# A shifted-window attention and convolution block on one core: maximum of the scores issued ahead of the normalization steps on DVE, probability copy issued ahead of exp on ACT

## The chip, the core and the metric

One core of a Trainium2 chip runs the whole program in one launch. The time is the device time in microseconds. The kernel before took 3653.8 us as the median of three runs (3641.2 to 3657.81). The engines are PE (matrix products, with PEld as its weight loads), DVE (vector), ACT (scalar functions and copies), POOL (a second elementwise engine) and SP, which only issues DMA transfers. Each works through its own list of instructions in the order written, and semaphores hold an instruction until another engine's work is done.

## The reference

For each of 32 images of 56 x 56 x 128 values:

```python
x = x + swin_attention(group_norm(x))   # 7x7 windows shifted by 3, 8 heads of 16 channels
x = x + conv3x3(group_norm(x))          # weights: scaled signs times a pruning mask

# inside the attention, for each of the 64 windows of 49 tokens
q, k, v = split(tokens @ qkv_weight.T + qkv_bias)
attn = softmax(q @ k.T / 4 + relative_position_bias + shift_mask)
out  = (attn @ v) @ proj_weight.T + proj_bias
```

## The kernel before

An image has 8 rows of 8 windows. A row is cut into 4 units, one for each pair of heads, so that an image has 32 units and the program runs 32 x 32 = 1024 of them. Every engine's list is written as a loop over images and, in it, over the unit number `u` from 0 to 31. What an engine does in a step of that loop is fixed by `u`; several images are in work at once: the attention of one, the convolution and the second normalization of the one before, and the loads and the first normalization of the next.

One unit `g` goes through these stations. PE forms the scores of two units together (`scores`, L908). DVE adds the bias into `s_sb` (L766, waits for `scores_ready`) and takes the row maximum `s_max` (L771). POOL subtracts it (L443). ACT takes exp into `probs` (L498, in the step after), PE turns it (`probsT_ps`, L919, two steps after), ACT copies the turned probabilities out of PSUM (`probsT`, L505, the same step as the turn). `probs` has two buffers, so exp of a unit also waits until the unit two before it has been turned.

One row of windows then closes a loop over engines. Let s0, s1, s2, s3 be the steps with `u % 4` equal to 0, 1, 2, 3.
- In s1, at its end, PE does the projection of a row (`misc_ps`, L895, needs `oT_lo`) and then `values` of the next row: 64 products with `v` (L932) and 32 sums of probabilities (L936), both into `attn_ps`. `values` needs the last `probsT` copy of its row (L505), which ACT makes in the same s1.
- In s2 PE goes on with `scores` of two units, and DVE takes the reciprocal of the sums (`recip`, L746, needs `attn_ps`). SP writes `recip` to DRAM (L366) and reads it back spread over partitions into `recip_wide` (L371).
- In s0, DVE multiplies into `o_sb` (L751, needs `recip_wide`), ACT forms the high half `oT_hi` (L548), and in s1 DVE forms the low half `oT_lo` (L759). That lets the projection go.

Around these stand, in fixed steps, DVE's low halves for the convolution and for the tokens (`plane_lo`, L778; `tok_lo`, L856), the sums of the convolution (L787 to L848), statistics, and the addition of the projection to `x` (L809), which waits for PE. ACT's list in a step is exp, then in s2 `m_1` of the convolution (L539), then the `probsT` copy, then the rest (`oT_hi`, copies of q, k, v, of loads and stores). No scheduler is at work: an engine does the next thing of its list or waits.

## Time and profile before

| | before |
|---|---|
| median of three runs | 3653.8 us (3641.2 to 3657.81) |
| the profiled execution | 3636.98 us |
| its span | 3635.2 us |
| PE busy | 3190.5 us (88%) |
| DVE busy | 3073.1 us (85%) |
| ACT busy | 2555.1 us (70%) |
| POOL busy | 2365.1 us (65%) |
| granted TensorE clock | 0.983 |

The span is what lies between the first and the last recorded instruction; the profiled execution's own time is 1.8 us longer. A busy share is a mean over all stages and over all of the span. Idle time in front of an instruction is put down to what released it. In the middle of the span the work repeats from image to image: the products of L932 for the same row of windows start at 1854.34 us and again at 1961.12 us, which is 106.78 us for an image.

### The profile page before, as it was taken

The numbers are of one execution on the slowest core, as the hardware profiler recorded it, in microseconds if no ns is written. First come the engines' busy times: TensorE is split into PE (matmuls) and PEld (weight loads), VectorE is DVE, ScalarE is ACT, GpSimd is POOL, SyncE is SP. The second block draws the span as 40 slices with busy tenths as digits, with TensorE's granted clock in tenths as the row PEclk, the third lists the DMA queues.
The fourth block names the chain that finished last, engine by engine and source line by source line (L and its number), as shares of the span: only waits on it lengthen the run. The fifth ranks groups of instructions, "written<-read, shape, count | busy, mean of one in ns | idle before, by whom it ended". The sixth has DMA issues, their size and how long they took to land.

```text
span 3635.2 us, 155064 instructions
## 1 busy us (share of the span) xinstructions
PE 3190.5 (88%) x64395; PEld 2684.8 (74%) x64395; DVE 3073.1 (85%) x6399; ACT 2555.1 (70%) x5729; POOL 2365.1 (65%) x3683
## 2 busy tenths in 40 slices
PE   2889989889899899898899999889898899898896
PEld 1667777777777777777777777777777777787775
DVE  5689888888888888888888888888888898888895
ACT  1667777767677777777777777777677777777772
POOL 4466666766667666667766667766667666667763
PEclk9999999999999999999999999999999999999998
DMA  2111111111111111111111111111111111111111
GB/s 57 37 42 52 47 42 47 49 50 49 37 47 50 49 52 47 42 47 50 52 52 50 42 45 49 50 52 50 37 47 50 50 52 47 42 47 50 34 35 36
DMA packets 260489, 169.26 MB, mean 47 GB/s; under 512 B 23120, under 2 KB 259792, under 8 KB 259792
## 3 DMA queue, kind: packets, MB, share of 16 engines
q1 hardware_dynamic: 259792, 159.34, 15.9%
q8 instruction: 514, 8.42, 1.0%
q14 instruction: 183, 1.50, 0.1%
HBM read 104.69 MB, written 54.59 MB: 44 GB/s over the span
## 4 chain that ended last, share of the span: by engine, by line
PE 33%; DVE 32%; issue 13%; POOL 9%; DMA 8%; ACT 4%; SPq 0%; DVEq 0%; ACTq 0%; POOLq 0%
PE conv_ps L1014 8%; DVE s_sb L766 6%; PE qkv_ps L895 6%; DMA recip_wide<-recip_dram 5%; PE attn_ps L932 4%; PE scores_ps L908 4%; PE attn_ps L936 4%; DVE plane_lo L778 3%; POOL s_sb L443 3%; DVE s_max L771 3%; DMA recip_dram<-recip 3%; DVE oT_lo L759 3%; PE probsT_ps L919 3%; DVE tok_lo L856 3%; DVE recip L746 2%
## 5 line engine op out<-in xcount | busy, mean ns | idle before, releaser
L443 POOL TENSOR_TENSOR s_sb<-s_sb,s_max 113x392 f32<-113x392 f32 x1024 | 998.9, 975 | 1092.7 <-DVE s_max L771 1091.4
L505 ACT COPY probsT<-probsT_ps 128x392 f32<-128x392 f32 x1024 | 490.8, 479 | 376.6 <-PE probsT_ps L919 366.4
L498 ACT ACTIVATE probs<-s_sb 113x392 f32<-113x392 f32 x1024 | 552.4, 539 | 221.1 <-POOL s_sb L443 218.6
L470 POOL TENSOR_TENSOR plane<-x_n 128x224 f32<-128x224 f32 x896 | 656.4, 753 | 18.7
L919 PE MATMUL probsT_ps<-ident,probs 113*128 113x113 f32 x4096 | 585.0, 265 | 38.7 <-ACT probsT L505 35.3
L771 DVE TENSOR_REDUCE s_max<-s_sb 113x8 f32<-113x392 f32 x1024 | 574.9, 561 | 35.3
L766 DVE TENSOR_TENSOR s_sb<-scores_ps,bias 113x392 f32<-113x392 f32 x1024 | 565.8, 552 | 41.0 <-PE scores_ps L908 37.1
L569 ACT COPY v<-qkv_ps 64x256 f32<-64x256 f32 (+2 forms) x1280 | 391.0, 325 | 211.6 <-PE qkv_ps L895 205.5
L1014 PE MATMUL conv_ps<-plane_hi,wc_hi 128*128 128x224 f16 x2688 | 484.4, 263 | 23.1 <-DVE conv_y L840 19.0
L919 PEld LDWEIGHTS probsT_ps<-ident,probs 113*128 113x128 f32 x4096 | 433.5, 141 | 90.7 <-ACT probs L498 47.9
L908 PE MATMUL scores_ps<-k,q 32*49 32x98 f32 x16384 | 477.4, 252 | 19.7 <-issue 19.4
L1014 PE MATMUL conv_ps<-plane_hi,wc_lo 128*128 128x224 f16 x2688 | 479.4, 261 | 0.0
L1014 PE MATMUL conv_ps<-plane_lo,wc_hi 128*128 128x224 f16 x2688 | 410.1, 262 | 34.9 <-DVE plane_lo L778 34.9
L908 PEld LDWEIGHTS scores_ps<-k,q 32*49 32x49 f32 x16384 | 365.6, 121 | 90.4 <-issue 32.6
L895 PE MATMUL qkv_ps<-wT_hi,tok_hi 128*128 128x128 f16 (+1 forms) x2304 | 395.6, 226 | 3.7 <-ACT v L569 1.9
L895 PE MATMUL qkv_ps<-wT_hi,tok_lo 128*128 128x128 f16 (+1 forms) x2304 | 389.1, 220 | 1.7 <-issue 1.7
L895 PE MATMUL qkv_ps<-wT_lo,tok_hi 128*128 128x128 f16 (+1 forms) x2304 | 389.1, 220 | 0.4 <-issue 0.3
L932 PEld LDWEIGHTS attn_ps<-probsT,v 128*32 128x32 f32 x16384 | 208.5, 113 | 218.5 <-ACT probsT L505 190.6
L932 PE MATMUL attn_ps<-probsT,v 128*32 128x49 f32 x16384 | 244.8, 213 | 129.7 <-ACT probsT L505 128.8
L482 POOL TENSOR_SCALAR x_n<-x,gn_y,gn_shift 128x371 f32<-128x371 f32 (+2 forms) x576 | 347.4, 613 | 7.6 <-POOL gn_shift L432 7.6
L746 DVE RECIPROCAL recip<-attn_ps 128x98 f32<-128x98 f32 x256 | 195.7, 765 | 162.9 <-PE attn_ps L936 162.6
L560 ACT ACTIVATE k<-qkv_ps,k_bias,k_scale 128x392 f32<-128x392 f32 x512 | 322.9, 687 | 4.5 <-PE qkv_ps L895 4.4
(144 smaller groups left out, 6799.1 us busy)
## 6 DMA issues: line engine op xcount, KB each, us to landing
x_in<-in_x_dram SPq DMA_DIRECT2D x224, 224.0 KB, 3.9
recip_wide<-recip_dram SPq DMA_DIRECT2D x256, 196.0 KB
out_dram<-x_out SPq DMA_DIRECT2D x224, 224.0 KB, 2.3
recip_dram<-recip SPq DMA_DIRECT2D x256, 12.2 KB, 1.7
x<-in_L_conv_w_dram SPq DMA_DIRECT2D x1, 576.0 KB
x<-L_conv_pruning_mask_dram SPq DMA_DIRECT2D x1, 576.0 KB
x_n<-_conv_rel_pos_table_dram SPq DMA_DIRECT2D x14, 10.7 KB
x_n<-in_mask_dram SPq DMA_DIRECT2D x1, 196.0 KB
```

Of the source, the lines that this page charges most:

```text
L443: nc.gpsimd.tensor_tensor(s, s, top, ALU.subtract).then_inc(sub_ready, 1)
L470: last = nc.gpsimd.tensor_tensor(plane[:, t % 2, j], *sums[j])
L498: nc.scalar.activation(probs[0:QP, slot % 2, :, :, 0:N], s_sb[0:QP, slot % 4], ACT.Exp)\
L505: nc.scalar.copy(probsT[:, g % PT_SLOTS], probsT_ps[:].rearrange("p (w n) -> p w n", n=ODD)[:, :, 0:N])\
L569: last = nc.scalar.copy(v[half, slot, w0:w0 + n, :, e * HD:(e + 1) * HD], vals[half, b:b + n, :, e, :])
L766: vec.tensor_tensor(s_sb[0:QP, u % 4].rearrange("p w h m -> p (w h m)"), scores_ps[0:QP, u % 2, 0:WP * 2 * N], bias[0:QP, edge, u % PAIRS] ...
L771: vec.tensor_reduce(s_max[0:QP, u % 4], s_sb[0:QP, u % 4].rearrange("p w h m -> p (w h) m"), AX.X, ALU.max).then_inc(max_ready, 1)
L895: last = mm(out_ps, w, t, start=(n == 0), stop=(n == 2))
L908: last = mm(scores_ps[p0:p0 + N, (u + n) % 2, (w // 2) * 2 * N:(w // 2 + 1) * 2 * N], q[at, r % 2, w, :], k[at, r % 2, w].rearrange("p e m ...
L919: last = nc.tensor.transpose(probsT_ps[:, w * 128:w * 128 + QP], probs[0:QP, u % 2, w].rearrange("p e m -> p (e m)"), ident[0:QP, 0:QP])
L932: mm(attn_ps[parts, w * N:(w + 1) * N], v[:, row % 2, w, pair, :], probsT[:, (row * PAIRS + pair) % PT_SLOTS, w, :], start=True, stop=True)
L1014: last = mm(conv_ps[:, j, 0:PP].rearrange("p (r w) -> p r w", w=W), w[:, j * KW + dx, :], p[:, j, k * TPAIRS:(k + 1) * TPAIRS, dx:dx + W], ...
```

## The change

On DVE, the two instructions of a unit's scores (bias and maximum) now stand at the head of each step, and the reciprocal (in s2), the product (in s0) and the low half (in s1) behind them. On ACT, the copy of the turned probabilities stands at the head of each step, ahead of exp and of `m_1`. No instruction is added or removed, and PE's, POOL's and SP's lists are the same.

```diff
--- before.py
+++ after.py
@@ -525,6 +525,8 @@
 
             def body(i):
                 for u in range(UNITS):
+                    if live(i, 0 if u >= LAG_T else -1):
+                        evacuate_probsT(i, i * UNITS + (u - LAG_T), u - LAG_T)
                     if live(i, 0 if u >= 1 else -1):
                         exp_unit(i, i * UNITS + (u - 1), u - 1)
                     for t in range(TILES):
@@ -538,8 +540,6 @@
                                 act.wait_ge(scaled_bias_ready, 1)
                             nc.scalar.activation(m_1[:], conv_ps[:, 1, 0:PP], ACT.Identity, bias=scaled_bias[:])\
                                 .then_inc(m1_ready, 1)
-                    if live(i, 0 if u >= LAG_T else -1):
-                        evacuate_probsT(i, i * UNITS + (u - LAG_T), u - LAG_T)
                     row = row_of(i, u, NORMED_AT)
                     if row is not None:
 
@@ -738,25 +738,6 @@
             def body(i):
                 for u in range(UNITS):
 
-                    row = row_of(i, u, VALUES_AT + 1)
-                    if row is not None:
-
-                        dve.wait_ge(attn_ready, row + 1)
-                        need(dve, recip_out, 16 * row)
-                        vec.reciprocal(recip[:], attn_ps[:, RT:RT + SUM_COLS]).then_inc(recip_ready, 1)
-                    row = row_of(i, u, NORMED_AT)
-                    if row is not None:
-
-                        dve.wait_ge(recip_wide_in, 16 * (row + 1))
-                        vec.tensor_tensor(o_sb[:].rearrange("p r (w c) -> p w r c", c=WIN),
-                                          attn_ps[:, 0:RT].rearrange("p (w r c) -> p w r c", r=WIN, c=WIN),
-                                          recip_wide[:].rearrange("p (w r c) -> p w r c", r=WIN, c=WIN), ALU.mult)\
-                            .then_inc(o_ready, 1)
-                    row = row_of(i, u, SPLIT_AT)
-                    if row is not None:
-
-                        dve.wait_ge(oT_hi_ready, row + 1)
-                        vec.tensor_tensor(flat(oT_lo), flat(o_sb), flat(oT_hi), ALU.subtract).then_inc(oT_lo_ready, 1)
                     if live(i):
 
                         g = i * UNITS + u
@@ -770,6 +751,25 @@
                         dve.wait_ge(biased, g + 1)
                         vec.tensor_reduce(s_max[0:QP, u % 4], s_sb[0:QP, u % 4].rearrange("p w h m -> p (w h) m"),
                                           AX.X, ALU.max).then_inc(max_ready, 1)
+                    row = row_of(i, u, VALUES_AT + 1)
+                    if row is not None:
+
+                        dve.wait_ge(attn_ready, row + 1)
+                        need(dve, recip_out, 16 * row)
+                        vec.reciprocal(recip[:], attn_ps[:, RT:RT + SUM_COLS]).then_inc(recip_ready, 1)
+                    row = row_of(i, u, NORMED_AT)
+                    if row is not None:
+
+                        dve.wait_ge(recip_wide_in, 16 * (row + 1))
+                        vec.tensor_tensor(o_sb[:].rearrange("p r (w c) -> p w r c", c=WIN),
+                                          attn_ps[:, 0:RT].rearrange("p (w r c) -> p w r c", r=WIN, c=WIN),
+                                          recip_wide[:].rearrange("p (w r c) -> p w r c", r=WIN, c=WIN), ALU.mult)\
+                            .then_inc(o_ready, 1)
+                    row = row_of(i, u, SPLIT_AT)
+                    if row is not None:
+
+                        dve.wait_ge(oT_hi_ready, row + 1)
+                        vec.tensor_tensor(flat(oT_lo), flat(o_sb), flat(oT_hi), ALU.subtract).then_inc(oT_lo_ready, 1)
                     t, half = divmod(u - VLO_AT, 2)
                     if 0 <= t < TILES and live(i, -1):
 
```

The first place is DVE, in a stretch of s0, s1 and s2 of one row: from the step that makes the product `o_sb` to the step that takes the reciprocal of the next row. Before:

```order
L751 TENSOR_TENSOR o_sb<-attn_ps,recip_wide 128x8x7x7 [waits recip_wide_in]
L766 TENSOR_TENSOR s_sb<-scores_ps,bias 113x392 [waits probs_ready,scores_ready]
L771 TENSOR_REDUCE s_max<-s_sb 113x8 [waits biased]
L778 TENSOR_TENSOR plane_lo<-plane,plane_hi 128x2x4x56 [waits plane_hi_ready]
L759 TENSOR_TENSOR oT_lo<-o_sb,oT_hi 128x392 [waits oT_hi_ready]
L766 TENSOR_TENSOR s_sb<-scores_ps,bias 113x392 [waits probs_ready,scores_ready]
L771 TENSOR_REDUCE s_max<-s_sb 113x8 [waits biased]
L778 TENSOR_TENSOR plane_lo<-plane,plane_hi 128x2x4x56 [waits plane_hi_ready]
L809 SCALAR_TENSOR_TENSOR x<-misc_ps,w_max,x 128x7x53 [waits misc_ready]
L809 SCALAR_TENSOR_TENSOR x<-misc_ps,w_max,x 128x7x3
L815 BN_STATS gn_stats<-x 128x6 [waits misc_free]
L746 RECIPROCAL recip<-attn_ps 128x98 [waits recip_out,attn_ready]
```

And the same stretch of the changed kernel, with the two instructions of s2 that now stand ahead of the reciprocal left to the second place:

```order
L747 TENSOR_TENSOR s_sb<-scores_ps,bias 113x392 [waits probs_ready,scores_ready]
L752 TENSOR_REDUCE s_max<-s_sb 113x8 [waits biased]
L764 TENSOR_TENSOR o_sb<-attn_ps,recip_wide 128x8x7x7 [waits recip_wide_in]
L778 TENSOR_TENSOR plane_lo<-plane,plane_hi 128x2x4x56 [waits plane_hi_ready]
L747 TENSOR_TENSOR s_sb<-scores_ps,bias 113x392 [waits probs_ready,scores_ready]
L752 TENSOR_REDUCE s_max<-s_sb 113x8 [waits biased]
L772 TENSOR_TENSOR oT_lo<-o_sb,oT_hi 128x392 [waits oT_hi_ready]
L778 TENSOR_TENSOR plane_lo<-plane,plane_hi 128x2x4x56 [waits plane_hi_ready]
L809 SCALAR_TENSOR_TENSOR x<-misc_ps,w_max,x 128x7x53 [waits misc_ready]
```

The product and the low half each moved behind the bias and maximum of their step; between the low half and the addition to `x`, which waits for the projection, the two score instructions are gone.

The second place is DVE at the reciprocal, in s2 of the row that follows. Before:

```order
L815 BN_STATS gn_stats<-x 128x6 [waits misc_free]
L746 RECIPROCAL recip<-attn_ps 128x98 [waits recip_out,attn_ready]
L766 TENSOR_TENSOR s_sb<-scores_ps,bias 113x392 [waits probs_ready,scores_ready]
L771 TENSOR_REDUCE s_max<-s_sb 113x8 [waits biased]
L787 TENSOR_TENSOR m_sum<-m,conv_ps 128x224 [waits conv_sums,m1_ready]
```

Now:

```order
L815 BN_STATS gn_stats<-x 128x6 [waits misc_free]
L747 TENSOR_TENSOR s_sb<-scores_ps,bias 113x392 [waits probs_ready,scores_ready]
L752 TENSOR_REDUCE s_max<-s_sb 113x8 [waits biased]
L759 RECIPROCAL recip<-attn_ps 128x98 [waits recip_out,attn_ready]
L787 TENSOR_TENSOR m_sum<-m,conv_ps 128x224 [waits conv_sums,m1_ready]
```

The reciprocal waits for the sums, which PE finishes ahead of the scores; it now stands behind the instruction that waits for the scores.

The third place is ACT in s1 and s2 of the same image. Before:

```order
L498 ACTIVATE probs<-s_sb 113x8x49 [waits probsT_ready,sub_ready]
L505 COPY probsT<-probsT_ps 128x392 [waits attn_ready,probsT_ready]
L560 ACTIVATE k<-qkv_ps,k_bias,k_scale 128x8x49 [waits qkv_ready]
L560 ACTIVATE k<-qkv_ps,k_bias,k_scale 128x8x49
L498 ACTIVATE probs<-s_sb 113x8x49 [waits probsT_ready,sub_ready]
L539 ACTIVATE m<-conv_ps,scaled_bias 128x224 [waits conv_sums,conv_half]
L505 COPY probsT<-probsT_ps 128x392 [waits attn_ready,probsT_ready]
```

Now:

```order
L505 COPY probsT<-probsT_ps 128x392 [waits attn_ready,probsT_ready]
L498 ACTIVATE probs<-s_sb 113x8x49 [waits probsT_ready,sub_ready]
L560 ACTIVATE k<-qkv_ps,k_bias,k_scale 128x8x49 [waits qkv_ready]
L560 ACTIVATE k<-qkv_ps,k_bias,k_scale 128x8x49
L505 COPY probsT<-probsT_ps 128x392 [waits attn_ready,probsT_ready]
L498 ACTIVATE probs<-s_sb 113x8x49 [waits probsT_ready,sub_ready]
L541 ACTIVATE m<-conv_ps,scaled_bias 128x224 [waits conv_sums,conv_half]
```

The copy no longer stands behind exp and `m_1`, and these two stand behind the copy's wait for the turn on PE.

## Rows read from the trace of the kernel before

**Rows 1.** The page's busy times: engine, us (share of the span), instructions.

```profile
PE 3190.5 (88%) x64395; PEld 2684.8 (74%) x64395; DVE 3073.1 (85%) x6399; ACT 2555.1 (70%) x5729; POOL 2365.1 (65%) x3683
```

**Rows 2.** The page's chain that ended last, shares of the span by engine.

```profile
PE 33%; DVE 32%; issue 13%; POOL 9%; DMA 8%; ACT 4%; SPq 0%; DVEq 0%; ACTq 0%; POOLq 0%
```

**Rows 3.** The waits: who <- whom: us in total, times, longest.

```profile
ACT probsT L505 <- PE probsT_ps L919: 366.4, 227, 3.4
...
DVE recip L746 <- PE attn_ps L936: 162.6, 105, 4.3
PE attn_ps L932 <- ACT probsT L505: 128.8, 69, 3.4
...
DVE o_sb L751 <- DMA recip_wide<-recip_dram: 103.0, 78, 3.5
...
PE misc_ps L895 <- DVE oT_lo L759: 23.5, 56, 2.6
```

**Rows 4.** Stretches between starts of L932: length, busy us (instructions), clock, DMA.

```profile
1854.34:1867.43 13.09, 11.09 (x239) 8.92 (x239) 9.07 (x17) 9.80 (x23) 12.17 (x24) 1.00 0.21 56
1867.43:1881.50 14.07, 13.71 (x269) 11.96 (x269) 13.35 (x28) 12.39 (x29) 13.14 (x16) 1.00 0.37 91
1881.50:1896.28 14.78, 13.04 (x259) 10.88 (x258) 14.00 (x28) 11.47 (x26) 12.02 (x16) 1.00 0.20 56
1896.28:1911.58 15.30, 12.12 (x255) 10.56 (x255) 13.46 (x32) 8.86 (x21) 12.00 (x27) 1.00 0.11 32
1911.58:1923.94 12.36, 12.05 (x252) 10.35 (x252) 10.49 (x19) 10.45 (x24) 8.84 (x13) 1.00 0.13 38
1923.94:1936.51 12.57, 12.12 (x253) 10.27 (x252) 12.36 (x24) 9.84 (x23) 7.04 (x11) 1.00 0.13 38
1936.51:1948.41 11.90, 11.90 (x253) 10.41 (x253) 9.80 (x21) 8.42 (x20) 4.18 (x5) 1.00 0.13 39
1948.41:1961.12 12.71, 10.92 (x239) 8.91 (x238) 11.98 (x34) 8.44 (x20) 3.80 (x8) 1.00 0.13 38
```

**Rows 5.** Timeline of DVE, fifth stretch: start, us, instruction, idle before.

```profile
1913.24 0.77 DVE L746 RECIPROCAL recip<-attn_ps 128x98 f32<-128x98 f32 x1 [3.09 <-PE attn_ps L936]
1914.05 0.57 DVE L766 TENSOR_TENSOR s_sb<-scores_ps,bias 113x392 f32<-113x392 f32 x1
...
1915.42 1.14 DVE L856 TENSOR_TENSOR tok_lo<-x_n,tok_hi 128x392 f16<-128x392 f32 x1
...
1922.00 1.21 DVE L759 TENSOR_TENSOR oT_lo<-o_sb,oT_hi 128x392 f16<-128x392 f32 x1
```

**Rows 6.** Timeline of PE: the projection of the fifth stretch; `values` after the eighth.

```profile
1923.35 0.33 PE L895 MATMUL misc_ps<-oT_hi,wT_hi 128*128 128x392 f16 x1 [0.31 <-DVE oT_lo L759]
...
1961.12 0.92 PE L932 MATMUL attn_ps<-probsT,v 128*32 128x49 f32 x64 [0.86 <-ACT probsT L505]
```

**Rows 7.** Timeline of DVE, first stretch.

```profile
1856.01 0.77 DVE L746 RECIPROCAL recip<-attn_ps 128x98 f32<-128x98 f32 x1 [1.02 <-PE attn_ps L936]
...
1862.46 0.57 DVE L751 TENSOR_TENSOR o_sb<-attn_ps,recip_wide 128x392 f32<-128x392 f32 x1 [1.85 <-DMA recip_wide<-recip_dram]
...
1864.01 0.69 DVE L778 TENSOR_TENSOR plane_lo<-plane,plane_hi 128x448 f16<-128x448 f32 x1
```

**Rows 8.** Timeline of DVE, seventh stretch.

```profile
1938.50 0.76 DVE L746 RECIPROCAL recip<-attn_ps 128x98 f32<-128x98 f32 x1
...
1944.60 0.57 DVE L751 TENSOR_TENSOR o_sb<-attn_ps,recip_wide 128x392 f32<-128x392 f32 x1 [0.62 <-DMA recip_wide<-recip_dram]
...
1946.15 0.56 DVE L759 TENSOR_TENSOR oT_lo<-o_sb,oT_hi 128x392 f16<-128x392 f32 x1
```

**Rows 9.** Timeline of POOL and of ACT, end of the fourth stretch.

```profile
1902.66 1.15 POOL L443 TENSOR_TENSOR s_sb<-s_sb,s_max 113x392 f32<-113x392 f32 x1 [0.26 <-DVE s_max L771]
...
1910.62 0.54 ACT L498 ACTIVATE probs<-s_sb 113x392 f32<-113x392 f32 x1 [0.26 <-POOL s_sb L443]
1911.06 0.46 ACT L505 COPY probsT<-probsT_ps 128x392 f32<-128x392 f32 x1
```

More of the change, by code:

```diff
@@ L739, in body @@
                 for u in range(UNITS):
+                    if live(i):
+                        g = i * UNITS + u
+                        dve.wait_ge(scores_ready, g + 1)
+                        need(dve, probs_ready, g - 3)
+                        edge = int(u // PAIRS == ROWS - 1)
+                        vec.tensor_tensor(s_sb[0:QP, u % 4].rearrange("p w h m -> p (w h m)"),
+                                          scores_ps[0:QP, u % 2, 0:WP * 2 * N],
+                                          bias[0:QP, edge, u % PAIRS].rearrange("p w h m -> p (w h m)"), ALU.add)\
+                            .then_inc(biased, 1)
+                        dve.wait_ge(biased, g + 1)
+                        vec.tensor_reduce(s_max[0:QP, u % 4], s_sb[0:QP, u % 4].rearrange("p w h m -> p (w h) m"),
+                                          AX.X, ALU.max).then_inc(max_ready, 1)
                     row = row_of(i, u, VALUES_AT + 1)
@@ L759, in body @@
                         vec.tensor_tensor(flat(oT_lo), flat(o_sb), flat(oT_hi), ALU.subtract).then_inc(oT_lo_ready, 1)
-                    if live(i):
-                        g = i * UNITS + u
-                        dve.wait_ge(scores_ready, g + 1)
-                        need(dve, probs_ready, g - 3)
-                        edge = int(u // PAIRS == ROWS - 1)
-                        vec.tensor_tensor(s_sb[0:QP, u % 4].rearrange("p w h m -> p (w h m)"),
-                                          scores_ps[0:QP, u % 2, 0:WP * 2 * N],
-                                          bias[0:QP, edge, u % PAIRS].rearrange("p w h m -> p (w h m)"), ALU.add)\
-                            .then_inc(biased, 1)
-                        dve.wait_ge(biased, g + 1)
-                        vec.tensor_reduce(s_max[0:QP, u % 4], s_sb[0:QP, u % 4].rearrange("p w h m -> p (w h) m"),
-                                          AX.X, ALU.max).then_inc(max_ready, 1)
                     t, half = divmod(u - VLO_AT, 2)
```

## The prediction, made before the changed kernel was run

> **What bounds the kernel now.** I read the busy shares first: PE 88%, DVE 85% [rows 1]. Neither is full, so something passes between them. The chain of waits says the same: 33% PE, 32% DVE, 8% DMA [rows 2]. Then the list of waits, for the places at which the change touches two engines. DVE waits at the reciprocal for the sums 105 times of 256 (162.6 us); PE waits at `values` for the probability copy (128.8 us); DVE waits at the product for the transfer of the reciprocals (103.0 us, 78 times); PE waits at the projection for the low half 56 times, though only for 23.5 us [rows 3]. Last the stretches of one image, cut at the starts of `values` [rows 4]; I call them A to H. They add to 106.78 us. The reader is to see that no one engine bounds them all: PE is busy for the whole of G (11.90 of 11.90), DVE for nearly all of F (12.36 of 12.57), and D, the longest, has neither full.
>
> All of them share one loop: sums on PE, reciprocal on DVE, DRAM and back, product, low half, projection, and `values` again. The change moves three links of that loop behind two instructions each, so I price the loop first and go through the stretches after it.
>
> **The durations.** With t the start of `values`:
> - t to the start of bias in s2 is 2.47 (1911.58 to 1914.05) when DVE isn't late; the reciprocal of 0.77 stands inside that gap, at t + 1.66, while PE is still at the scores [rows 4, 5]. In A it is 1856.01, t + 1.67 [rows 7].
> - o_sb, bias and maximum take 1.55 from start to start, in A (1862.46 to 1864.01) and in G (1944.60 to 1946.15). A product takes about 0.48 of it before the next starts, an estimate from its 0.57, so bias and maximum take 1.07 [rows 7, 8].
> - From the end of the reciprocal to the product, where the product really waited, 5.68 in A (1856.78 to 1862.46) and 5.34 in G (1939.26 to 1944.60) [rows 7, 8].
> - From the end of the low half to the next `values`, where PE waited for it, 0.73 (1923.21 to 1923.94) [rows 4 to 6].
> - The low half takes 0.56 in G and 1.21 in E [rows 5, 8].
>
> **The change, part by part.**
>
> 1. Reciprocal behind bias and maximum (s2). Where DVE came early, the reciprocal used PE's 0.8 us at the scores. Now DVE idles through that gap, and the reciprocal ends at t + 2.47 + 1.07 + 0.77 = t + 4.31 instead of t + 2.43: 1.88 later. Nothing hides this for the transfer.
>
> 2. Product behind bias and maximum (s0). Where the product waits for the transfer, the two now run inside that wait: -1.07 for what follows them, nothing for the product.
>
> 3. Low half behind bias and maximum (s1). The projection comes 1.07 later where PE waits for it. Bias and maximum used to cover DVE's wait for the projection; now DVE has nothing (or one `plane_lo`) there.
>
> So the loop through the transfer is at least 2.47 + 1.07 + 0.77 + 5.34 + 1.55 + 0.56 + 0.73 = 12.49, and 12.8 to 13.4 with 5.68 or with a `plane_lo` or `tok_lo` in s0. The loop through DVE's work is what DVE does from bias of s2 to the end of the low half, plus 0.73 + 2.47 = 3.20 for projection, `values` and scores, under which only the 1.3 to 1.9 us of additions and statistics fit. Before, all of DVE's work fitted.
>
> 4. Whether DVE and POOL hold each other up. `oT_lo` takes 1.21 just after POOL has begun a subtraction and 0.56 otherwise, and `tok_lo` 1.14 [rows 5, 8]. Behind its own unit's maximum, `oT_lo` starts before POOL does, as it does in G; so I take 0.65 off in C and E and 0.58 off E's `tok_lo` in s2, which the reciprocal now parts from the maximum. E's `tok_lo` in s0 moves behind the product, while POOL subtracts: +0.35, an estimate (0.84 of subtraction less 0.48). The Trainium skill has this as a rule (page "SBUF — State Buffer", section "Who interferes with whom"): a DVE instruction with two SBUF inputs and a reading GpSimd instruction exclude each other, and the first to issue decides who waits. By that rule these savings are sure; without it E and C would be 0.9 and 0.6 slower still. The trace agrees, with 0.56 against 1.21.
>
> 5. The copy ahead of exp. At the end of D the copy stood behind exp, which waited 0.26 for POOL and held it 0.44 more (1910.62 to 1911.06) [rows 9]: -0.70. At the end of H `values` waited 0.86 for the copy [rows 6]: -0.86. Of PE's 128.8 us at this wait [rows 3] the rest, up to 3.2 us an image, is the wait for POOL's normalization in D, and stays. The price: in s2 exp and `m_1` now stand behind ACT's wait for the turn (366.4 us in all [rows 3]). That puts them about 0.8 to 2 us later. Exp of that unit is needed a whole step later, and `m_1` only by a DVE that is itself later, so I cost it at nothing but in B, where ACT also serves PE's input tiles through one buffer. If that cover is gone, each row pays up to 0.4.
>
> **The sum, stretch by stretch.**
> - A (13.09): the product starts at t + 4.31 + 5.68 = t + 9.99, before it was t + 8.12. Bias and maximum are then done, so `plane_lo`, for which PE's convolution waits, starts at t + 10.47 instead of t + 9.67. +0.8.
> - B (14.07): DVE busy 13.35, of it 1.9 behind the low half: 13.2 to 13.35 - 1.9 + 3.2 = 14.5 to 14.65. +0.5.
> - C (14.78): DVE busy 14.00; the gap of 0.8 is added, 0.65 comes off the low half. +0.2.
> - D (15.30): bounded by POOL, whose last subtraction before the normalization waits for a DVE maximum [rows 9]; this comes 0.7 later, and the copy gives 0.70 back. 0.
> - E (12.36): bias to end of the low half was 9.16; with reciprocal 0.77, bias and maximum 1.07, less 0.65 and 0.58, plus 0.35, 10.1. 2.47 + 10.1 + 0.73 = 13.3. +0.95.
> - F (12.57): the same work, but here DVE came late to the reciprocal, so part of the gap was idle for it already; both loops give about 13.1. +0.5.
> - G (11.90): the transfer loop, 12.49. +0.6.
> - H (12.71): the loop through DVE gives 12.9 (busy 11.98 less about 2.3 of additions and statistics, plus 3.2), after the 0.86 is used up. +0.2.
>
> Together +3.75 us an image, 32 images: +120 us. The profiled execution took 3636.98, so the changed one should take 3757. The median of the runs is 3653.8, 17 above that execution, which gives 3774. I say 3768.
>
> **The rivals.**
> - ACT's order costs too: exp and `m_1` late in s2 hold up PE's next turn or the input tiles' buffer in most rows, 0.4 us x 256 = 100 more: 3870. For it: 366.4 us of waiting in front of the copy. Against it: the need of those results is a step away. 0.13.
> - Faster. The low half and the product have slack on PE (only 23.5 us of waiting in 56 of 256 rows), the scores get to POOL, ACT and `values` sooner, and what is left is part 5 (1.56 x 32 = 50) and some of part 4: 3595. It would need the 1.07 at the low half to be covered by PE's other work in nearly all rows, and it decides the sign from the point where the projection would have waited anyway. Against it: PE already waits there in E, and G's PE has no gap to give. 0.07.
> - The rows take up most of the delays. DVE comes late to the reciprocal in 151 of 256 rows, so it loses no gap there, and part 5 balances the rest: 3650 to 3690, centre 3665. 0.15, of which half is within 0.5%.
> - That the lists don't move as said can't be: the order shows it.
>
> **How the numbers follow.** The forecast (3700 to 3820) has 0.65, the larger loss 0.13, the absorbed one 0.15, the faster one 0.07. The range leaves out the faster case and the far part of the larger loss: 3665 to 3840. A difference below 0.5% (18 us) can't be told from none here. Slower: 0.65 + 0.13 + half of 0.15, about 0.86; within 0.5% 0.07; faster 0.07.
>
> **What would show it.** Right: DVE's bias instruction now waits for the scores in over 100 rows, with some 0.6 to 0.8 us each; the wait of the projection for the low half grows from 23.5 us to over 100; DVE's wait for the projection grows; the reciprocal waits for nothing; the product waits for the transfer in more rows, A and G among them; PE's wait at `values` falls by 30 to 50 us; `oT_lo` takes near 0.6 on average. E and G are longer by 0.6 to 1. Wrong: if the projection hardly waits for the low half, part 3 is wrong and the time is near that of before; if PE's wait at the turns grows, part 5 was priced too low.

## The result, and the profile after

The changed kernel takes 3911.95 us (median of four runs, 3899.91 to 3914.53) against 3650.52 of before: 1.071 times as long, 95% interval 1.068 to 1.075. The forecast was slower, with 3768 us in a range of 3665 to 3840; the loss is 261 us where about 120 were forecast. The profiled execution's span is 3898.1 us.

The page's busy times and chain by engine, after [rows 1, 2]:

```profile
PE 3250.1 (83%) x64395; PEld 2674.6 (69%) x64395; DVE 3105.9 (80%) x6399; ACT 2494.3 (64%) x5729; POOL 2352.6 (60%) x3683
...
PE 31%; DVE 30%; DMA 16%; issue 13%; POOL 6%; ACT 5%; SPq 0%; ACTq 0%; DVEq 0%; POOLq 0%
```

No instruction was added, and what every engine is busy with changed by 2.4% or less; the engines wait more, and DMA's share of the chain doubled from 8% to 16%. The waits after (who <- whom: us in total, times, longest) [rows 3]:

```profile
ACT probsT L505 <- PE probsT_ps L919: 659.9, 391, 4.0
ACT oT_hi L548 <- DVE o_sb L764: 443.1, 256, 8.6
DVE s_sb L747 <- PE scores_ps L908: 278.7, 246, 4.5
...
PE qkv_ps L895 <- ACT q L557: 217.1, 164, 4.5
DVE x L809 <- PE misc_ps L895: 175.8, 185, 2.2
DVE o_sb L764 <- DMA recip_wide<-recip_dram: 167.9, 113, 4.0
...
PE conv_ps L1014 <- DVE plane_lo L778: 91.0, 31, 4.2
...
PE attn_ps L932 <- ACT probsT L505: 45.8, 30, 1.6
...
PE misc_ps L895 <- DVE oT_lo L772: 14.3, 45, 2.6
```

DVE now waits for the scores 246 times, in 207 of the 256 rows; before it was 49 times and 37.1 us. The wait of the projection for the low half did not grow: PE waits at qkv for the q copy instead (26.9 us before), and every high half on ACT waits for the product (38.6 us in all before).

Stretches A to H of one image, cut at the starts of `values` (length, busy us of PE, PEld, DVE, ACT, POOL, granted clock, DMA) [rows 4]:

```profile
1985.07:2000.50 15.43, 12.82 (x240) 9.62 (x239) 10.36 (x18) 11.29 (x26) 14.62 (x26) 0.89 0.22 61
2000.50:2015.71 15.21, 13.87 (x269) 11.91 (x268) 13.90 (x26) 10.92 (x26) 10.27 (x13) 1.00 0.36 84
2015.71:2031.75 16.04, 13.04 (x259) 10.88 (x259) 14.41 (x30) 10.81 (x26) 12.67 (x16) 1.00 0.20 51
2031.75:2047.41 15.66, 12.70 (x256) 10.41 (x255) 14.40 (x32) 8.76 (x22) 10.81 (x24) 1.00 0.11 31
2047.41:2061.87 14.46, 12.06 (x252) 10.28 (x252) 10.53 (x20) 10.32 (x25) 10.60 (x16) 1.00 0.08 22
2061.87:2077.13 15.26, 12.86 (x253) 10.60 (x252) 11.31 (x23) 10.85 (x25) 6.53 (x10) 0.95 0.15 42
2077.13:2092.02 14.89, 12.85 (x253) 11.11 (x253) 9.71 (x20) 7.25 (x18) 3.62 (x4) 0.94 0.07 21
2092.02:2104.93 12.91, 11.12 (x239) 8.87 (x238) 11.24 (x32) 7.55 (x19) 3.90 (x10) 1.00 0.11 32
```

Every stretch is longer than its partner of before, H by 0.20 only, and three of them have a clock below 1.00. One image turned out to be a poor sample, so the table gives medians over 30 images, those at the full clock (2.4 GHz) apart from those with at least 0.3 us at half clock (1.2 GHz). It is worked out from the starts of L932 and the granted clock of each profiled execution. The two rows of means take all 30 images, whatever their clock.

| | A | B | C | D | E | F | G | H |
|---|---|---|---|---|---|---|---|---|
| before, full clock | 13.08 | 14.08 | 14.78 | 15.30 | 12.37 | 12.57 | 11.90 | 12.72 |
| after, full clock | 13.86 | 15.23 | 16.03 | 15.38 | 13.83 | 13.34 | 12.86 | 12.75 |
| difference | +0.78 | +1.15 | +1.25 | +0.08 | +1.46 | +0.77 | +0.96 | +0.03 |
| forecast | +0.8 | +0.5 | +0.2 | 0 | +0.95 | +0.5 | +0.6 | +0.2 |
| images with half clock, before | 2 | 0 | 0 | 1 | 20 | 0 | 0 | 1 |
| images with half clock, after | 22 | 6 | 4 | 1 | 3 | 6 | 6 | 3 |
| their median, after | 15.84 | 15.52 | 17.59 | 16.59 | 14.47 | 14.67 | 14.98 | 13.94 |
| mean, before | 13.47 | 14.20 | 14.88 | 15.41 | 13.48 | 12.86 | 12.24 | 12.72 |
| mean, after | 15.67 | 15.34 | 16.24 | 15.54 | 14.03 | 13.81 | 13.51 | 13.03 |

At the full clock the eight differences add to 6.48 us an image, 207 us over 32 images; the means differ by 7.91, which is 253 us. The forecast row adds to 3.75.

In stretch A, DVE and then PE (start, us, instruction, idle before) [rows 7]:

```profile
1987.54 0.57 DVE L747 TENSOR_TENSOR s_sb<-scores_ps,bias 113x392 f32<-113x392 f32 x1 [1.00 <-PE scores_ps L908]
...
1988.62 0.76 DVE L759 RECIPROCAL recip<-attn_ps 128x98 f32<-128x98 f32 x1
...
1994.78 0.57 DVE L764 TENSOR_TENSOR o_sb<-attn_ps,recip_wide 128x392 f32<-128x392 f32 x1 [2.12 <-DMA recip_wide<-recip_dram]
```

```profile
1996.18 0.46 PE L1014 MATMUL conv_ps<-plane_lo,wc_hi 128*128 128x224 f16 x3 [2.54 <-DVE plane_lo L778]
...
1997.53 0.53 PE L895 MATMUL qkv_ps<-tok_hi,wT_hi 128*128 128x392 f16 x1
1997.86 0.53 PE L895 MATMUL qkv_ps<-tok_lo,wT_hi 128*128 128x392 f16 x1
```

With t = 1985.07 the product starts at t + 9.71 (forecast 9.99, before 8.12), and PE stands idle for 2.54 us. Behind it the products of 392 columns start 0.33 us apart and take 0.53; at the full clock they start 0.17 us apart and take 0.33, as the one in [rows 6]. That is the half clock. Images that have it take a median of 15.84 us in A against 13.86 without it, another 2 us.

### The profile page after: what moved, and what is told of

Read it like the earlier page. It is cut to its first block, busy times and chain, and to the rows that moved or that the text cites. A ratio compares the mean times of both kernels' runs of the same rounds, so it can differ in the third digit from the quotient of the medians.

```text
span 3898.1 us, 155063 instructions
## 1 busy us (share of the span) xinstructions
PE 3250.1 (83%) x64395; PEld 2674.6 (69%) x64395; DVE 3105.9 (80%) x6399; ACT 2494.3 (64%) x5729; POOL 2352.6 (60%) x3683
## 4 chain that ended last, share of the span: by engine, by line
PE 31%; DVE 30%; DMA 16%; issue 13%; POOL 6%; ACT 5%; SPq 0%; ACTq 0%; DVEq 0%; POOLq 0%
DMA recip_wide<-recip_dram 10%; DVE s_sb L747 7%; DMA recip_dram<-recip 6%; PE scores_ps L908 6%; PE attn_ps L932 6%; PE attn_ps L936 5%; PE conv_ps L1014 4%; PE misc_ps L895 4%; DVE recip L759 4%; DVE plane_lo L778 4%; PE qkv_ps L895 3%; DVE s_max L752 3%; DVE o_sb L764 3%; DVE tok_lo L856 2%; ACT q L557 2%
## 5 line engine op out<-in xcount | busy, mean ns | idle before, releaser
L443 POOL TENSOR_TENSOR s_sb<-s_sb,s_max 113x392 f32<-113x392 f32 x1024 | 941.1, 919 | 1366.8 <-DVE s_max L752 1362.6
L505 ACT COPY probsT<-probsT_ps 128x392 f32<-128x392 f32 x1024 | 498.8, 487 | 669.1 <-PE probsT_ps L919 659.9
L470 POOL TENSOR_TENSOR plane<-x_n 128x224 f32<-128x224 f32 x896 | 667.7, 765 | 18.7
L1014 PE MATMUL conv_ps<-plane_lo,wc_hi 128*128 128x224 f16 x2688 | 418.8, 266 | 91.0 <-DVE plane_lo L778 91.0
L908 PE MATMUL scores_ps<-k,q 32*49 32x98 f32 x16384 | 463.0, 248 | 15.0 <-issue 13.4
L548 ACT CAST oT_hi<-o_sb 128x392 f16<-128x392 f32 x256 | 132.6, 518 | 443.1 <-DVE o_sb L764 443.1
L908 PEld LDWEIGHTS scores_ps<-k,q 32*49 32x49 f32 x16384 | 355.5, 119 | 82.4 <-issue 26.2
L778 DVE TENSOR_TENSOR plane_lo<-plane,plane_hi 128x448 f16<-128x448 f32 x448 | 388.5, 867 | 10.8 <-ACT plane_hi L589 10.4
L895 PE MATMUL qkv_ps<-tok_hi,wT_hi 128*128 128x392 f16 x512 | 179.0, 350 | 224.3 <-ACT q L557 217.1
L809 DVE SCALAR_TENSOR_TENSOR x<-misc_ps,w_max,x 128x371 f32<-128x371 f32 (+2 forms) x576 | 199.7, 393 | 175.9 <-PE misc_ps L895 175.8
```

The lines of the kernel that those rows point to most:

```text
L443: nc.gpsimd.tensor_tensor(s, s, top, ALU.subtract).then_inc(sub_ready, 1)
L470: last = nc.gpsimd.tensor_tensor(plane[:, t % 2, j], *sums[j])
L505: nc.scalar.copy(probsT[:, g % PT_SLOTS], probsT_ps[:].rearrange("p (w n) -> p w n", n=ODD)[:, :, 0:N])\
L778: vec.tensor_tensor(plane_lo[:, two, at, 1:W + 1], plane[:, t % 2, two], plane_hi[:, two, at, 1:W + 1], ALU.subtract).then_inc(plane_lo_re ...
L895: last = mm(out_ps, w, t, start=(n == 0), stop=(n == 2))
L908: last = mm(scores_ps[p0:p0 + N, (u + n) % 2, (w // 2) * 2 * N:(w // 2 + 1) * 2 * N], q[at, r % 2, w, :], k[at, r % 2, w].rearrange("p e m ...
```

## The experiments

Each kernel was timed in the same rounds as the kernel before, which took 3639.5 to 3646.6 us in them. Two times from different rounds differ by that spread too, so a difference between two changed kernels is best read from their costs over the kernel before of their own rounds. Stretch times are medians at the full clock, as in the table above, unless it says otherwise; a stretch is called halved in an image where it has at least 0.3 us at half clock. Orders on DVE are written with S for bias and maximum, R for the reciprocal, P for the product, L for the low half: before is R P L S, the change S R P L.

**e1 to e4: the two engines apart, the high half, the clock.**

```diff
 e1   DVE: S R P L; ACT as before
 e2   DVE: R P L S; ACT: copy ahead of exp in every step
```

> DVE's part of the change alone: bias and maximum ahead of reciprocal, product and low half; ACT's list as in the kernel before (exp, then the copy). Theory (the loss is DVE's part: the product now comes later, and on ACT the high half waits for it and holds what is queued behind it): about 3900 to 3960 us, since the copy's gain at values, up to 50 us, is gone too; ACT's wait for the product stays near 440 us in all. Rival (ACT's new order is what costs, exp standing behind the wait for the turn): below 3720 us.

Measured: 3972.89 us, 1.0886 (1.0859 to 1.0912), a little over what was expected. DVE's part costs 326 us; the copy then gives some 61 back. The changed kernel differs from this one by ACT's order alone. B and C take 15.23 and 16.04 here and 15.23 and 16.03 there, so on top of DVE's moves the copy costs them nothing. D falls from 16.17 to 15.38 by it, and E is halved in 3 images instead of 24, though at the full clock E and F rise by 0.40 and 0.30 (from 13.43 and 13.04).

> ACT's part alone: the copy ahead of exp in every step; DVE's list as in the kernel before. Theory: the copy is ready earlier at values at the end of the stretches D and H, exp is needed a step later: 3590 to 3630 us against 3650 of before. Rival (ACT's order costs): 3700 us or more, with PE waiting for exp at the turns.

Measured: 3636.57 us, 0.9973 (0.9960 to 0.9985). H falls from 12.72 to 11.94 and D from 15.30 to 14.88, but B and C rise by 0.46 and 0.36 and E by 0.64 at the full clock. Its waits:

```profile
DVE m_sum L787 <- ACT m L541: 106.9, 199, 2.4
...
PE probsT_ps L919 <- ACT probs L498: 43.6, 69, 1.4
```

Before, DVE waited 9.5 us for `m_1`, and PE's wait for exp in that place was not among the waits of 6 us and more. The time lies in neither range that was expected, so both theories hold in part: the gain is there, and a price in B, C and E eats nearly all of it. With DVE's moves beside it most of that price is gone again: DVE's wait for `m_1` is 13.9 us in the changed kernel.

```diff
 e3, ACT, step s0, on the changed kernel
-   oT_hi copy, loads (MID), q/k/v copies, stores (END)
+   loads (MID), q/k/v copies, stores (END), oT_hi copy
```

> The changed kernel with one move on ACT: in s0 the high half oT_hi stands behind the copies of q, of loads and of stores (end of the step) and no longer ahead of them. Theory (the wait of oT_hi for the product holds the q copy and the store copy, and PE waits for these): PE's wait at qkv for the q copy falls from 217 us to under 50, its waits for x_out in B and C fall, stretches B, C, F, G and so the time fall by 60 to 130 us, to 3780 to 3850. Rival one (DVE and POOL hold each other up more, plane_lo taking 0.87 instead of 0.65): the time stays within 15 us of 3912. Rival two (the low half itself is late for the projection): stays, or gets longer by the later high half.

Measured: 3915.05 us, 1.0726 (1.0693 to 1.0759), no gain where 60 to 130 us were expected. The waits show why:

```profile
PE misc_ps L895 <- DVE oT_lo L772: 228.6, 191, 4.7
DVE o_sb L764 <- DMA recip_wide<-recip_dram: 164.5, 109, 4.0
```

PE's wait for the q copy is gone, and one of the same size has come at the projection. Product to high half to q copy to PE, and product to low half to projection, are two branches of one loop and about equally long. B fell to 14.89 and G to 12.46, which is the 12.49 of the prediction's loop, but E was halved in 14 images instead of 3. The queue on ACT is a branch, not the cause.

```diff
 e4, PE, on the changed kernel, ahead of the first wait for plane_lo of each image
+   for _ in range(16):
+       mm(conv_ps[:, 2:4, PP:256], ident[:], group[:, 0:64].rearrange("p (a c) -> p a c", a=2), start=True, stop=True)
```

> The changed kernel with 16 needless products on PE (64 columns each, into unused columns) issued just ahead of the first wait for plane_lo of each image, in stretch A, where PE stands idle for some 2.5 us. Theory (after that idle time the granted clock of TensorE halves, which costs A about 2 us in 22 of 30 images): the half-speed stretches in A go, A takes 13.9 us in most images, the time falls by 30 to 50 us to about 3870. Rival (the idle time alone is the price, and the clock is a by-stander): 3912 or slightly more.

Measured: 3889.95 us, 1.0675 (1.0657 to 1.0694). A was halved in 3 images, but took 14.61 at the full clock, since the products needed 3.70 us and not the 2.5 that were free. So e17 was made, with 10 of them.

> As the run with 16 needless products in A, but with 10, which take 2.3 us (0.23 us each there) and so fit into PE's idle time of 2.5 us. Theory: A at 13.9 us in nearly all images, half-speed stretches in A gone: 3855 to 3880 us, 15 to 25 below the run with 16. Rival (the idle time has to be filled to its end): A halves again in over 10 of 30 images and the time is 3890 or more.

Measured: 3874.71 us, 1.0629 (1.0592 to 1.0666), with more work on PE. That is 37 us below the changed kernel by the medians, and 30 by the two costs over the kernel before of their own rounds (232 and 261 us). A takes 13.92 in 21 images and is halved in 9; its mean falls from 15.67 to 14.89, which is 25 us over 32 images, while B to H stay within 0.05. So the 13 halvings of A that went were worth some 25 to 37 us, a fifth to a quarter of the 141 that the forecast lacked, and 9 are left.

**e5 to e7 and e9: each move alone, and the reciprocal put back.**

```diff
 e5   DVE: P L S R    (the reciprocal alone moved)
 e6   DVE: R L S P    (the product alone)
 e7   DVE: R P S L    (the low half alone)
 e9   DVE: R S P L, ACT: copy ahead of exp    (the change without the reciprocal)
```

In e5 to e7 ACT's order is the one of before.

> The kernel before with one of DVE's three moves: in s2 the reciprocal stands behind bias and maximum. Theory one (the loop through the transfer and through DVE's work, as forecast: the reciprocal ends 1.88 us later, and DVE idles 0.8 us for the scores): A +1.9 and more half-speed stretches there, B, C, D and E about +0.8 each, G +0.6: about 3840 us (3790 to 3880), the largest of the three moves by far. Rival (ACT's queue behind the high half, and the port shared with POOL, carry the loss): below 3720 us.

Measured: 4032.78 us, 1.1067 (1.1033 to 1.1102), worse than the whole change. At the full clock A takes 14.99 (+1.91), B +0.80, C +0.86, D +0.97, E +1.93, F +0.95, G 13.78 (+1.88). That is far over the 3790 to 3880 expected. Of the forecast 1.88, by which the reciprocal ends later, A and G show just as much:

```profile
DVE o_sb L745 <- DMA recip_wide<-recip_dram: 389.7, 220, 5.6
...
DVE s_sb L760 <- PE scores_ps L908: 350.9, 236, 5.5
```

In A the way is the one of the prediction's sum: product, `plane_lo`, the convolution on PE. In G it isn't the loop over the low half, so that its 1.88 is in part luck. There the product starts at t + 9.98 instead of t + 8.02, and the low half ends at t + 12.09; with the 0.73 of the prediction G would end near t + 12.8. It ends at t + 13.78, because bias and maximum of the unit behind the product come later with it, and that unit goes on through POOL and exp and holds the copy behind exp until t + 13.72. One such place (G of an image, timeline of all engines):

```profile
1912.86 0.56 DVE L753 TENSOR_TENSOR oT_lo<-o_sb,oT_hi 128x392 f16<-128x392 f32 x1
...
1914.15 0.54 ACT L498 ACTIVATE probs<-s_sb 113x392 f32<-113x392 f32 x1 [0.67 <-POOL s_sb L443]
...
1914.59 0.46 ACT L505 COPY probsT<-probsT_ps 128x392 f32<-128x392 f32 x1
...
1915.11 0.92 PE L932 MATMUL attn_ps<-probsT,v 128*32 128x49 f32 x64 [0.38 <-ACT probsT L505]
```

> The kernel before with the product alone behind bias and maximum of s0. Theory one: where the product waits for the transfer (A) the two now run inside that wait, about -1 us in A, elsewhere the same DVE work in another order: 3610 to 3660 us. Rival (the high half and, behind it, the q copy come 1.07 us later on ACT, and plane_lo, no longer right behind the maximum, meets POOL's subtraction): 3680 to 3740 us, with B and C longer.

Measured: 3644.38 us, 1.0007 (0.9996 to 1.0018). A falls to 12.36; B, C, H and E rise by 0.28, 0.19, 0.29 and 0.58.

> The kernel before with the low half alone behind bias and maximum of s1. Theory one (the projection comes later where PE waits for the low half, and DVE has nothing under the projection, against a low half that takes 0.56 instead of 0.87): E and F +0.4 to +0.8, others near 0: 3660 to 3730 us. Rival (plane_lo, now right behind the low half, waits for POOL): B and C longer by 0.5 or more, plane_lo's mean near 0.75 instead of 0.65 us.

Measured: 3672.92 us, 1.0077 (1.0061 to 1.0093). A is longer by 0.46 and E by 0.63, B and C are as before, though `plane_lo` takes 0.753 us on average: the rival's duration came, its cost didn't.

> The changed kernel with one part undone: the reciprocal stands ahead of bias and maximum in s2 again; product, low half and ACT's copy stay where the change put them. Theory (the reciprocal's place is what the transfer's loop, the wait for the scores and the idle time in front of the halved clock hang on): close to the kernel before, 3620 to 3690 us, the half-speed stretches in A gone. Rival (the three other moves carry a share of their own once they are together): 3750 us or more.

Measured: 3668.54 us, 1.0082 (1.0062 to 1.0102). That is 29 us over the kernel before of its rounds, so putting the reciprocal back recovers 232 of the 261 us. A is 12.38, G 11.90, and DVE's wait for the transfer nearly goes:

```profile
DVE s_sb L753 <- PE scores_ps L908: 55.9, 63, 3.2
DVE o_sb L764 <- DMA recip_wide<-recip_dram: 19.1, 26, 2.9
```

The clock has a share in this. At the full clock the stretches of e9 are still 2.91 us an image longer than before (93 us over 32 images; B 0.80, C 0.74, E 1.46, F 0.76), against 6.48 (207 us) for the whole change. Most of the 93 is not seen in the time, as E is no longer halved in any image and the half-clock time of the run is 33 us instead of 127. So at the full clock the reciprocal's place carries over half of the loss, 114 of 207 us, and the rest of what it recovers is clock.

Alone, the moves cost 390, 1 and 30 us. In e1, with the product behind bias and maximum too, the reciprocal's 1.9 in A and G shrinks to 0.92 and 1.16: this fits part 2 of the prediction, the two instructions inside the wait for the transfer.

**e8, e12 and e18: versions that the runs point to.** The conditions on the first and last images are left out here.

```diff
 e8, ACT, on the kernel before
+   if u % PAIRS == 1: evacuate_probsT(...)      (ahead of exp)
    exp_unit(...)
    m_1
+   if u % PAIRS != 1: evacuate_probsT(...)      (as before)
 e12  e8, the product behind bias and maximum at u = 12 alone, and 12 needless products
      ahead of the wait of values at the end of D
 e18  e8, the 12 products in D, and 3 ahead of the first wait for plane_lo in A
```

> The kernel before with the copy ahead of exp in s1 alone (the step in which values waits for it); in the other steps exp and m_1 come first as before. Theory (in s2 the copy's wait for the turn holds exp, m_1 and the input tile's copy, which costs B, C and E 0.4 to 0.6 us each in the run with ACT's part alone; in s1 it only gains): H stays at 11.9 and D at 14.9, B and C go back to 14.1 and 14.8: 3600 to 3620 us, 20 to 30 below the run with ACT's part alone. Rival (B and C lose for another reason): the same time as with ACT's part alone, 3637.

Measured: 3560.43 us, 0.9777 (0.9760 to 0.9795), more than expected. H takes 11.78, D 14.51, B and C 14.07 and 14.77 as before; E is halved in 10 images instead of 20, since PE's wait for the copy at the end of D got shorter (74.2 us in 31 waits, where D and H together had 128.8).

> Built from what the runs showed, on the kernel before: the copy ahead of exp in s1 alone; the product behind bias and maximum only in the step of A (u = 12), where it waits for the transfer; and 12 needless products on PE just ahead of the wait of values at the end of D, where PE idles some 2.5 us. Theory: 3560 from the run with the copy alone, less 0.7 us in A (22 us) and less 1.5 us in the 10 of 30 images whose E runs at half speed (15 us): 3515 to 3545 us. Rival (A's gain goes to B, and the clock falls elsewhere): 3560 or more.

Measured: 3548.24 us, 0.9759 (0.9730 to 0.9789), just short of what was expected. E is at the full clock in all images, but A stays at 13.22 and is halved in 9. The product's move gained nothing there: `plane_lo` starts at t + 9.41 instead of t + 9.63, but takes 1.09 us instead of 0.85, and PE's products with it start at t + 10.56 in e8 and e12 alike. The difference to e8 lies inside the intervals.

> The copy ahead of exp in s1 alone, with 12 needless products ahead of the wait of values at the end of D and 3 ahead of the first wait for plane_lo in A; the product stays where it was before. Theory: E at full speed in all images (-15 us against 3560), A halved in fewer than the 9 of 30 images of the combined run: 3535 to 3550 us. Rival: the clock halves elsewhere and the time is 3560.

Measured: 3567.97 us, 0.9799 (0.9772 to 0.9827), a miss: no better than e8. A takes 13.55 at the full clock, 0.3 more than without the three products, and is still halved in 6 images; they saved no more than they cost.

**e10, e11, e13 to e16: with POOL's reads or the transfers taken away.**

```diff
 e10 (before), e11 (changed)
-   last = nc.gpsimd.tensor_tensor(plane[:, t % 2, j], *sums[j])
+   last = nc.gpsimd.memset(plane[:, t % 2, j], 1.0)
 e13 (before), e14 (changed)
-   nc.gpsimd.tensor_tensor(s, s, top, ALU.subtract).then_inc(sub_ready, 1)
+   nc.gpsimd.memset(s, 0.0).then_inc(sub_ready, 1)
 e15 (before), e16 (changed)
-   both DMAs of a row on SP, and DVE's two waits for them
+   recip_wide filled once with a constant
```

> The kernel before with POOL's sums for the convolution (plane<-x_n, L470) replaced by a fill of the same tiles with a constant, which reads nothing from SBUF; this leaves out the input transform of the convolution. Theory: plane_lo near 0.61 to 0.65 us as before, POOL less busy: 3590 to 3650 us. It is the partner of the next run.

> The changed kernel with POOL's sums for the convolution replaced in the same way (the input transform is left out). Theory one (the order on DVE makes plane_lo wait for POOL's reads, 0.87 instead of 0.65 us, which is why B and C lost 1.15 and 1.25 instead of the forecast 0.5 and 0.2): plane_lo's mean falls to 0.70 or less, B and C lose less against the partner run, the difference to it shrinks from 261 to 200 to 230 us. Rival (plane_lo's wait is beside the path): the difference stays 250 to 270 us.

Measured: 3625.90 and 3861.09 us, 235 apart, which is in neither of the ranges expected. `plane_lo` stayed at 0.849 us in e11, B and C lost the same 1.15 and 1.29. The sums were not what holds `plane_lo`, so this pair did not test whether DVE and POOL hold each other up.

> The kernel before with POOL's subtraction of the maximum (L443) replaced by a fill with zeros, which reads nothing; this leaves the scores out of the softmax. Theory: oT_lo falls from 0.87 to about 0.6 us, since the subtraction no longer holds it, and POOL's stretch D gets shorter: 3540 to 3630 us. Partner of the next run.

> The changed kernel with the same replacement. Theory one (plane_lo at 0.87 us waits for the subtraction that its own step's maximum has let go, and this carries half of what B and C lost beyond the forecast): plane_lo at 0.65 us or less, B and C lose 0.5 us less against the partner run than 1.15 and 1.25. Theory two (B and C lose the reciprocal's 0.8 us of waiting for the scores, plus ACT's order, and the port is beside the path): plane_lo at 0.65 us too, but B and C still lose 1.0 or more against the partner.

Measured: 3543.60 and 3845.87 us, 302 apart. `plane_lo` over all, with the kernel before first, the changed kernel second and e14 third (busy, mean ns):

```profile
L778 DVE TENSOR_TENSOR plane_lo<-plane,plane_hi 128x448 f16<-128x448 f32 x448 | 293.1, 654 | 10.8 <-ACT plane_hi L589 10.5
```

```profile
L778 DVE TENSOR_TENSOR plane_lo<-plane,plane_hi 128x448 f16<-128x448 f32 x448 | 388.5, 867 | 10.8 <-ACT plane_hi L589 10.4
```

```profile
L778 DVE TENSOR_TENSOR plane_lo<-plane,plane_hi 128x448 f16<-128x448 f32 x448 | 318.9, 712 | 10.8 <-ACT plane_hi L589 10.8
```

So it is the subtraction that holds it, for 0.155 of the 0.213 us. Yet B and C lose 1.33 and 1.58 against the partner, not less: theory two stands. For C the kernels one by one say more. Without the subtraction C is 0.67 us shorter before (14.78 to 14.11) and only 0.34 shorter after (16.03 to 15.69). So the change took away about half of what the subtraction costs C, not all of it. B is 14.08 in both kernels of before, so it had nothing to save there. One thing blurs this: the fill takes 0.43 us and the subtraction 0.92 to 0.98, so it also hands its result on sooner.

> The kernel before without the two transfers of the reciprocals: the product takes a constant tile and waits for no transfer (the normalization of the attention is left out). Theory: only A and G's DVE waits go, PE bounds the same stretches: 3570 to 3640 us. Partner of the next run.

> The changed kernel without the two transfers, in the same way. Theory (A and G grow through the loop over the transfer, which starts 1.88 us later; B to F through DVE's own waits): A and G fall back by 0.7 us or more each against their growth of 0.8 and 1.0, and the half-speed stretches in A go, so that the difference to the partner is 130 to 190 us instead of 261. Rival (all of it is DVE's waiting for the scores and the projection): the difference stays above 230 us.

Measured: 3614.23 and 3682.84 us, 69 apart instead of 261. In e16 A takes 11.67 and G 11.90, both at the full clock in all 30 images, and the wait of the convolution for `plane_lo` in A is short (L1000 and L764 here, 91.0 us in the changed kernel):

```profile
DVE s_sb L735 <- PE scores_ps L894: 258.9, 238, 5.1
...
PE conv_ps L1000 <- DVE plane_lo L764: 11.6, 27, 0.7
```

B, C and F keep their +1.45, +1.26 and +0.77 without any transfer, and E +1.48. They run through DVE's own waits, and its 259 us of waiting for the scores are still there. By the times, the transfers carry some three quarters of the loss. But E is halved in 27 images of e15 and in none of e16, which flatters e16. At the full clock the two are 3.80 us an image apart, 122 us over 32 images against 207, so there the transfers carry about two fifths.

## Why the prediction was right in its direction and wrong in its size

- The loop (parts 1 and 2) was right in A. The reciprocal starts 1.88 us later there (t + 3.55, before t + 1.67), the product at t + 10.04 at the full clock for a forecast of t + 9.99, and the stretch grew by 0.78 for 0.8. Where the reciprocal moved alone (e5), A grew by 1.91. That G's 1.88 in e5 agrees is in part luck, as said there. e9 and e16 show that the reciprocal's place and the transfer behind it carry the largest part of the loss.
- The failed step is the sum stretch by stretch. It came out at 3.75 us an image, where the means of 30 images give 7.91. Its terms were mis-sized as follows (us over the 30 images, measured for forecast): A 66 for 24, C 41 for 6, G 38 for 18, B 34 for 15, F 28 for 15, H 9 for 6, D 4 for 0, E 17 for 28.
- A, the largest part, was priced by its wait alone. The longer wait is followed by a half clock in 22 of 30 images, at 2 us each (e17, with 13 halvings fewer, takes 0.78 off A's mean): over these 30 images A costs 66 us (404.2 to 470.2 us). The half-clock time of the whole run rose from 127 to 197 us. No rival held this.
- C is the term most mis-sized at the full clock: +1.25 for +0.2. I had taken 0.65 off for a quicker low half. It came on average (0.564 us, from 0.874), but `plane_lo` paid it back to the same subtraction (0.867 from 0.654; 95 us in all, against 79 saved), and e13 and e14 put the saving in C at about 0.33. The gap at the scores and the product show 0.86 and 0.19 there alone (e5, e6), and without the subtraction C pays 1.58; what makes up the rest is not settled.
- B came to +1.15 for +0.5. The reciprocal and the product alone show 0.80 and 0.28 there (e5, e6), the low half nothing (e7). The product's move, which the forecast had at nothing but a gain, has a price where it doesn't wait for the transfer.
- G came to +0.96 instead of +0.6, 0.4 of it through the branch over the high half and the q copy on ACT (12.46 without it in e3), which the walk through the loop had left out.
- E was read from an untypical image. Its 12.36 is what 10 of 30 images take; the other 20 take 13.9 at half clock, since PE idles at the end of D. So E's +1.46 at the full clock became +0.56 in the mean. Of the 1.46 DVE's part makes 1.06 (13.43 in e1), near the forecast 0.95, and ACT's order the other 0.40.
- Part 4: `oT_lo` got quicker and `plane_lo` slower, and each is near its shorter time when POOL only fills (0.560 us for `oT_lo` in e13, 0.712 for `plane_lo` in e14). The Trainium skill's rule on the port (page "SBUF — State Buffer", section "Who interferes with whom"), that a DVE instruction with two SBUF inputs contends with a POOL instruction that reads SBUF and not with one that only writes, held in both directions, for `oT_lo` and for `plane_lo`. I had applied it to one of the two instructions that stand one behind the other.
- Part 5 depends on what stands beside it. On the kernel before (e2) the copy gives 0.78 in H and 0.42 in D, and its order costs B, C and E 0.46, 0.36 and 0.64, which e8 shows to lie all outside s1. On top of DVE's moves (the changed kernel against e1) it gives 0.79 in D for a forecast 0.70 and nothing in H. There it costs B and C nothing, and DVE waits 13.9 us for `m_1` instead of 106.9, as the forecast had argued (it had kept a little for B). It costs E and F 0.40 and 0.30, which the forecast left out. So the rival on ACT's order was right for E and F only.
- Of the signs to look for, the wait for the scores came (1.1 us each instead of 0.6 to 0.8), and so did DVE's wait for the projection (175.8 us, 50.5 before), the transfer's, in all rows of G and nearly all of A, and `values`' (83 us less instead of 30 to 50). The projection's wait for the low half fell to 14.3 us, where over 100 were forecast; its place was taken by PE's wait for the q copy, 217 us. The prediction had called a short wait there a sign that part 3 is wrong and the time near that of before. As the time was not, this sign was a bad one: e3 shows that the two waits stand for branches of about equal length.

## What to carry to other kernels

In a loop over several engines, count how much later each link ends, a transfer's start above all: the reciprocal, which had filled the wait for the scores, ended 1.88 us later behind that wait and two instructions, and everything behind its transfer with it. Give an instruction that another engine waits for the first place only in the step where that wait stands last (e8), since in the others it only puts its own wait in front of what is ready. Test a move both alone and with the others: the copy's price in B and C was there alone (e2) and gone beside DVE's moves (e1 against the change). And take stretches from many images, with the clock beside them, before one is used as the base of a sum; a run that changes the clock's halvings has to be compared at the full clock as well.

## What the runs showed of the hardware that was not expected

TensorE's clock fell to 1.2 GHz behind the idle time of one stretch and not of another, and a change of 1 to 2 us in that idle time moved it from E to A. At the end of D PE's wait was 3.17 us before (median of 30 images) and 1.64 after, and E was halved in 20 and in 3 images. In A PE's longest wait was 0.88 and 2.94 us, and A was halved in 2 and in 22. Needless products in the idle time kept it at 2.4 GHz in most images (A halved in 3 of 30 with 16 of them, in 9 with 10). In e9, where the waits at these two places were 1.64 and 1.14 us, the half-clock time of the whole run was 33 us. The length of one wait doesn't settle it: in e8 and e12 the longest wait in A is the same 1.44 us, and A is halved in 2 images and in 9.
